# A mixture-of-experts vision kernel: who waits for the landing of the scattered rows

## The reference

```python
h = tok(x, channel_weights)            # sums of 16 x 16 patches, then 12 -> 192: 196 tokens per image
h = h + attn(layernorm(h), ...)        # 12 heads of 16; relu(1 + qk + qk*qk/2), normalised, @ v, @ w_proj + b_proj
h = h + ffn(layernorm(h), ...)         # 8 experts, top 2 of a softmax router

# ffn, for each expert e:
w_e = sum(top_w * (top_i == e))
h   = gelu(flat @ w1[e] + b1[e])       # 192 -> 768
out = out + w_e * (h @ w2[e] + b2[e])  # 768 -> 192
```

## Time and profile before

| | |
|---|---|
| median of 3 runs | 1792.08 us (1792.0 to 1793.45) |
| profiled execution | 1789.12 us, of it a span of 1787.3 us from the first to the last instruction |
| TensorE busy | 1380.5 us, 77% |
| DVE busy | 975.3 us, 55% |
| POOL busy | 821.5 us, 46% |
| ACT busy | 632.7 us, 35% |
| mean granted TensorE clock | 0.863 |
| moved by DMA | 318.36 MB, 178 GB/s over the span |

### The profile page before, as it was taken

The page is one execution under the profiler, slowest core; times in us unless marked ns, Lnnn a source line. Parts: engine busy times, 40 slices in busy tenths (PEclk is TensorE's granted clock), DMA queues, the critical chain, the costliest instruction groups (busy, mean ns, idle before and its releaser), DMA issues.

```text
span 1787.3 us, 29130 instructions
## 1 busy us (share of the span) xinstructions
PE 1380.5 (77%) x7878; PEld 1223.5 (68%) x7878; DVE 975.3 (55%) x3625; ACT 632.7 (35%) x1161; POOL 821.5 (46%) x617
## 2 busy tenths in 40 slices
PE   5456642696969787877787778777788779999996
PEld 4345532585858676767676777677677668988886
DVE  2867776457474747474747565756563322332332
ACT  1112111243433333333333343434243435555553
POOL 0011333245444445454545454545455556666555
PEclk9975555698989888888888889888889889999998
DMA  6976886487787878787878787878753645566555
GB/s 161 245 207 177 215 211 184 118 218 205 180 212 175 215 176 222 173 228 172 219 172 210 176 228 183 218 173 218 177 146 78 178 108 130 134 146 144 124 133 137
DMA packets 232822, 318.36 MB, mean 178 GB/s; under 512 B 27173, under 2 KB 205078, under 8 KB 232790
## 3 DMA queue, kind: packets, MB, share of 16 engines
q1 hardware_dynamic: 187094, 274.97, 56.8%
q0 software_dynamic: 45696, 43.02, 14.9%
HBM read 261.19 MB, written 56.72 MB: 178 GB/s over the span
## 4 chain that ended last, share of the span: by engine, by line
PE 51%; POOL 17%; DVE 14%; issue 10%; DMA 5%; ACT 2%; SPq 1%; POOLq 0%; DVEq 0%; ACTq 0%
PE ps L904 17%; PE ps L879 16%; POOL rows_d L545 10%; POOL result L560 4%; DMA rows_d<-rows,sloti 4%; DVE red L948 4%; PE ps L708 3%; PE ps L828 3%; PE ps L852 3%; PE ps L853 3%; POOL w1l L568 3%; PE ps L817 2%; DVE topi L1074 1%; PE ps L902 1%; PE ps L776 1%
## 5 line engine op out<-in xcount | busy, mean ns | idle before, releaser
L904 PE MATMUL ps<-w2r,hid 128*128 128x192 f32 x2736 | 538.7, 339 | 0.0
L904 PEld LDWEIGHTS ps<-w2r,hid 128*128 128x128 f32 x2736 | 489.6, 200 | 30.3 <-issue 1.5
L560 POOL DMA_INDIRECT result<-ys,ridx x228 | 353.6, 1551 | 277.5 <-issue 143.0
L948 DVE TENSOR_REDUCE red<-xbuf 112x14 f32<-112x448 f32 x768 | 425.8, 606 | 35.2 <-PE ps L776 34.5
L545 POOL DMA_INDIRECT rows_d<-rows,sloti x256 | 246.3, 962 | 416.1 <-DVE sloti L1124 236.1
L656 ACT ACTIVATE hid<-ps,b1s 128x512 f32<-128x512 f32 x344 | 236.0, 686 | 370.7 <-PE ps L879 369.6
L568 POOL TENSOR_TENSOR w1l<-w1r,w1h 128x768 fp32r<-128x768 f32 x116 | 238.2, 2054 | 250.4 <-ACT w1h L666 250.1
L879 PE MATMUL ps<-xh,w1h 128*128 128x512 f32 x344 | 183.8, 534 | 119.2 <-POOL w1l L568 110.5
L1170 DVE TENSOR_TENSOR xl<-ps,xh 128x512 fp32r<-128x512 f32 x58 | 40.1, 691 | 257.5 <-ACT xh L672 257.5
L879 PEld LDWEIGHTS ps<-xh,w1h 128*128 128x128 f32 x344 | 68.3, 199 | 126.6 <-issue 119.5
L776 PE MATMUL ps<-cst,red 112*48 112x14 f32 x448 | 44.7, 251 | 129.0 <-DVE red L948 112.7
(11 more groups left out here) (168 smaller groups left out, 1891.5 us busy)
## 6 DMA issues: line engine op xcount, KB each, us to landing
xbuf<-x SPq DMA_DIRECT2D x128, 1176.0 KB, 10.4
w2r<-L_ffn_w SPq DMA_DIRECT2D x177, 192.0 KB, 3.9
xr<-rows_d SPq DMA_DIRECT2D x59, 402.0 KB
w1r<-L_ffn_w SPq DMA_DIRECT2D x59, 384.0 KB, 3.4
w1r<-L_ffn_w SPq DMA_DIRECT2D x118, 192.0 KB, 4.2
result<-h1s SPq DMA_DIRECT2D x32, 294.0 KB
rows_d<-rows,sloti POOLq DMA_INDIRECT x256
result<-ys,ridx POOLq DMA_INDIRECT x228, 5.0
```

Of the source, the lines that this page charges most:

```text
L560: pool.indirect_dma_start(out, bass.IndirectOffsetOnAxis(ap=ridx[:, b, n:n + 1], axis=0), ys[:, b, n, :], None, compute_op=ALU.add).then_i ...
L904: last = mm(yout(n), hid[:, m % 3, cols], w2r[:, b, m, :], start=False, stop=m == MC - 1 and n % 2 == 1)
L948: V.tensor_reduce(red[:, k // 2, CH * (k % 2) + c, :], xbuf[:, k % XSLOTS, c, :].rearrange("p (r j w) -> p j r w", r=2, j=G), AX.XY, ALU.a ...
```

## The change

POOL no longer waits at the end of `Q` and no longer raises the two semaphores, which go. Each of the four waiters now waits on the DMA semaphores `d_scat` and `d_h1` themselves: 256 of `d_scat` and 32 of `d_h1` for each step. In step 0 ACT and DVE have nothing to wait for; for that, step 0 is written out ahead of the loop of the prologue on every engine, which makes the program longer by one copy of the step without tiles.

```diff
         def schedule(eng, handlers, prime=None, before_tail=None):
 
-            with eng.Fori(0, PRO) as s:
+            tiles_do(eng, handlers, s=0, with_tiles=False)
+            with eng.Fori(1, PRO) as s:
                 tiles_do(eng, handlers, s=s, with_tiles=False)
...
+        def after_first(s):
+
+            return not isinstance(s, int) or s > 0
...
-                sp.wait_ge(s_listed, listed)
+                wait_first(sp, d_scat, listed * (32 * NT))
+                sp.wait_ge(d_h1, listed * 32)
                 w = d_rows[buf]
...
-            with sp.Fori(0, PRO) as s:
+            tiles_do(sp, handlers, s=0, with_tiles=False)
+            with sp.Fori(1, PRO) as s:
                 tiles_do(sp, handlers, s=s, with_tiles=False)
...
-                listed[0] = s + 1
+                listed[0] = s
...
-            pool.sem_inc(s_stored, 1)
-            pool.sem_inc(s_listed, 1)
...
-                if q == 3:
-                    pool.wait_ge(d_scat, s * (32 * NT) + 32 * NT)
-                    pool.wait_ge(d_h1, s * 32 + 32)
-                    pool.sem_inc(s_stored, 1)
-                    pool.sem_inc(s_listed, 1)
...
             def S8(s, q):
                 if q == 0:
-                    act.wait_ge(s_stored, s + 1)
+                    if after_first(s):
+                        act.wait_ge(d_h1, s * 32)
...
-                    act.wait_ge(s_listed, s + 1)
+                    if after_first(s):
+                        act.wait_ge(d_scat, s * (32 * NT))
...
             def S11(s):
 
-                dve.wait_ge(s_listed, s + 1)
+                if after_first(s):
+                    dve.wait_ge(d_scat, s * (32 * NT))
```

More of the change, by code:

```diff
@@ L311, in vit_layer @@
         s_res, s_h1 = sem("residual_ready"), sem("residual_copied")
-        s_stored = sem("residual_stored")
         s_gap, s_th, s_norm = sem("gap_ready"), sem("tanh_ready"), sem("rows_normalised")
@@ L315, in vit_layer @@
         s_slots = sem("slots_ready")
-        s_listed = sem("rows_listed")
         s_pick = sem("tile_picked")
@@ L488, in _ @@
             handlers = {"P": P, "L": L, "J": J, "K": K, "S10": S10}
-            with sp.Fori(0, PRO) as s:
+            tiles_do(sp, handlers, s=0, with_tiles=False)
+            with sp.Fori(1, PRO) as s:
                 tiles_do(sp, handlers, s=s, with_tiles=False)
             for j in range(2):
-                load_rows(j, j, PRO + 1, first=True)
+                load_rows(j, j, PRO, first=True)
                 load_w1(j, j, first=True)
@@ L508, in _ @@
             sp.wait_ge(d_pad, 32 + 16 * NE)
-            listed[0] = STEPS + 1
+            listed[0] = STEPS
             with sp.Fori(0, TAIL) as i:
```

## The result

The changed kernel takes 1729.53 us (median of 4 runs, 1725.22 to 1732.18), the kernel before 1792.04 us beside it (1788.08 to 1793.45): a ratio of 0.9652, 95% interval 0.9624 to 0.9681. The forecast was 1711 us with a range of 1690 to 1745. The profiled execution took 1726.95 us, 62.2 us less than the 1789.12 us of the one before.

The account below looks back on a forecast made before the run. The prediction took POOL's wait for the scatters' landing, ahead of the adds and w1l, as the bound. Terms 69.7 + 11.7 = 81.4 us off the profiled 1789.1 gave 1707.7, plus 3.0 for the median: 1711 us, range 1690 to 1745.

Parts of the forecast that it names:

- What bounds the kernel: Twelve steps with tiles: the last scatter's landing holds POOL's adds and w1l, so TensorE waits about 8.5 us each.
- POOL's two waits go: POOL, twelve places: first add follows the last scatter by 0.40 us, saving 69.7 us, ends 70.9 and 57.9.
- an idle time of the same length before the second add: Sign on POOL that the forecast is wrong: the 4 to 8 us idle time reappears before the second add.
- its lower end of 57.9: Least saving from POOL's wait, if the first add still came 1.38 us after release at twelve places.
- TensorE's clock: TensorE after the gaps: shorter gaps keep 2.4 GHz, five places at 2.33 us give 11.7 us, ends 0 and 25.6.
- the five that the forecast had under 1.9 us: Remaining TensorE gaps before w1l taken as short enough to keep the clock, below the halfway mark of 2.1 us.
- SP's, ACT's and DVE's own waits: These engines wait for scatters and stores themselves: 0 us taken, SP's estimated 6 us of added instructions hidden.
- step 0 outside the loop: Prologue: executing one written-out copy of the step costs 0, give or take 1 us.
- What would be late next: After the change: second tile's rows with 2 us slack, DMA engines with less time per step, last 21 tiles unchanged.
- The rows of the second tile: X0 of the second tile moves earlier to 543.3 us, its rows land by about 541, slack 2 us.
- the rival in which DMA becomes the bound: Earlier adds take turns from the loads, rows land 4 to 5 us later, half the gain lost: 1751 us; chance 0.15.
- The fit for a software-generated transfer: Scatter landing at about 2.0 us plus bytes over 436 GB/s: some 2.2 us, time about 1766 us; rejected for the trace.

Follow-up runs that it names:

- Experiment 1: Changed kernel with POOL's wait for the scatters' landing at the end of Q put back, without announcements: 1808.86 us, ratio 0.9985 to the kernel before.
- experiment 2: Kernel before with only step 0 written out ahead of the loops: 1813.42 us, ratio 1.0014 to the kernel before.
- experiment 10: Changed kernel with the first half of w1l ahead of the adds of A in steps with tiles, tail in old order: 1740.87 us, ratio 0.9622.
- experiment 11: Kernel before, POOL's wait and announcements kept, first half of w1l ahead of them in steps with tiles, tail in old order: 1740.08 us, ratio 0.9617.
- experiment 6: Changed kernel with the first half of the next tile's w1l ahead of the adds of A everywhere, tail included: 1774.91 us, ratio 0.9793.
- experiment 3: Kernel before with POOL's waits and announcements moved behind the next step's first W0, step 0 in its loop: 1771.13 us, ratio 0.9771.
- experiment 4: Changed kernel with eight more adds of zeros to padding rows posted by POOL ahead of step 0: 1790.85 us, ratio 0.9880 to the kernel before.
- experiment 5: Changed kernel run again, unaltered, on the second of the three later chips: 1759.45 us, ratio 0.9697 to the kernel before.
- experiment 8: Changed kernel with TensorE doing the eight matmuls of S4 twice in steps with tiles: 1784.79 us, ratio 0.9855 to the kernel before.
- experiment 9: Changed kernel run again, unaltered, on the third of the three later chips: 1762.47 us, ratio 0.9735 to the kernel before.
- experiment 12: Changed kernel with three more adds of zeros to padding rows ahead of step 0: 1766.47 us, ratio 0.9765 to the kernel before.

## Why the prediction was right, and where it was off

**What bounds the kernel** was read rightly: the landing of the scatters was in the chain of every step with tiles, and it left it. Experiment 1 puts the whole gain on that wait.

**"POOL's two waits go", 69.7 us.** The hand-over was 0.30 us, the lower end, so the term itself gave 70.9. But the step asked only what could hold the first add, and took the remaining three for granted. In three of the twelve places POOL paused before the second add, 12.8 us in all. The paragraph on signs to look for named "an idle time of the same length before the second add" as one that would speak against the forecast; it came in three steps of twelve. The term measured 58.1 us, which is next to its lower end of 57.9, for another reason than that end was drawn from. TensorE's wait for `w1l` was forecast to fall to about 40 us; it is 55.1, and the pauses are 12.8 of that.

**"TensorE's clock", 11.7 us.** It measured 4.1. This is the step that failed. It read a gap of 1.41 us as one that keeps the clock and one of 2.76 as one that loses it, both rightly, and drew the line halfway, at 2.1 us. But nothing in the rows spoke for the middle. Gaps of 1.50, 1.66, 1.80 and 2.33 us left the first matmul at 2.4 GHz, but behind the last three the clock fell nonetheless, 1.0 to 1.5 us into the work, and cost 1.7 us each (estimates, as in the table). Only the gap of 1.50 us cost nothing. The gap of 2.42 us cost 1.7 us too, and those of 2.8 to 3.1 us cost 2.7 to 2.9, more than most gaps of about 9 us did before (1.6 to 3.1). So a gap that was cut from 9 to 3 us gave nothing back of the clock, and could take more. The gaps were mis-sized too: of the five that the forecast had under 1.9 us (steps 5, 6, 7, 9 and 11) two came so, 1.66 and 1.50 us; the others were 3.04, 7.28 (a pause) and 2.76. The price of 2.33 us a gap was right: 28.1 us behind twelve gaps before is 2.34 each.

**SP's, ACT's and DVE's own waits, and step 0 outside the loop, 0 us.** Right: experiments 1 and 2, to within their intervals. SP's added instructions cost nothing that shows there either.

**What would be late next.** The rows of the second tile were not: TensorE's other waits in the step did not grow, DMA fell to 1% of the chain, and the rival in which DMA becomes the bound (1751 us) did not come. Per microsecond DMA moved more between `S1` of step 5 and `S1` of step 15, 209 GB/s against 196 (the kernel before first):

```profile
417.57:1331.66 914.09, 726.46 (x4251) 647.27 (x4251) 562.52 (x2111) 338.85 (x630) 450.24 (x341) 0.87 0.80 196
415.82:1275.39 859.57, 721.92 (x4250) 643.56 (x4250) 580.39 (x2111) 339.08 (x630) 451.11 (x341) 0.90 0.84 209
```

The fit for a software-generated transfer of the Trainium skill (DMA: Bandwidth & Descriptors, Anatomy of one DMA) would have made the wait worth 26 us; what went before the first adds was 70.9. The trace was the right guide, since it held the landing beside full DMA engines.

**The sum** was 81.4 us against 62.2: 11.6 of the 19.2 us are the pauses (69.7 to 58.1), 7.6 the clock. The 1.2 us won in the prologue and the 1.2 us by which the lines of the table exceed the measured gain cancel. Of the last, 0.3 us are in the stretch from the last of the twelve gaps to the end (342.9 us, before 342.5); where the rest is, no view showed.

**Of the other chips** the forecast says nothing, and there the gain was 46 to 55 us in place of 62. In the step, two waits lie one behind the other on TensorE: for DVE's `phi` before `S3` and then for `w1l`. Where the first is longer, less of the second is left to be won: in experiment 2 the wait for `w1l` is 75.9 us, on the chip of the result 110.5.

## What to carry to other kernels

A wait on an engine costs what is queued behind it and is needed soonest. Before removing one, ask which instruction behind it somebody waits for, and whether that instruction can go first: here 2 us of `w1l` moved ahead of the wait were worth at least as much as removing the wait (experiments 10 and 11). But that holds per stage: the same order cost a gap of 3.1 to 4.2 us in every three tiles of the tail, and the clock behind it, where the operand of the moved work was not ready (experiment 6). And when a wait leaves a train of several transfers, price the gaps between all of them, not only the one before the first.

## What the runs showed that was not expected

**POOL's posting of transfers can pause in the middle.** With scatters just posted and not waited for, POOL stood 2.6 to 5.4 us between the first and the second add behind them, in steps 7, 10 and 13, on all four chips, in the changed kernel and in experiments 3, 4, 5, 8, 9 and 12. With `w1l` between the scatters and the adds it was 2.02 us in step 7, 2.54 in step 10 and gone in step 13 in experiment 10, and 2.78, 2.58 and 1.15 us in experiment 6. With the wait in place there was none between two adds. What it waits for can be read from the packets of POOL's own queue (q0), here in step 10 of the changed kernel, in the windows 947:948, 948:949 and 949:950 us:

```profile
q0 software_dynamic: 103, 0.14, 64.9%
q0 software_dynamic: 132, 0.11, 63.6%
q0 software_dynamic: 11, 0.01, 5.0%
```

From 950 to 951 us this queue moves nothing, and the second add starts at 951.20. In windows of 0.25 us the last packets before the second add are 1.0, 1.2 and 1.3 us ahead of it in the three pauses. In experiment 3 they are within 0.4 us of it. In step 8, which has no pause, the queue still moves 9 to 14 packets in 0.25 us when the second add starts (775.69 us). So in those three steps POOL went on only when what it had posted was through or nearly so, and the later the adds begin, the less is left of that. DVE did the same instructions during the pause of step 7 as in step 8.

The kernel before has smaller hold-ups too. The first add of a tile that waits for ACT starts 0.8 us after the end of `ys`; for the tiles 6, 19 and 31 it is 2.2 to 2.3 us, and for tile 50, in the tail, 1.6, though POOL's wait on `d_add` at the head of `A` means that the adds of the tile before had landed, and no scatter was under way. The changed kernel has them at the same tiles (the 7.1 us of the waits above is at tile 6, with the wait for `ys` in it). Not the cause of the long pauses: the longer program and instruction loads (experiment 3), and the number of transfers or rows posted before (experiments 4 and 12). Why they come every third step, and there alone, stays open. Other data or another length of the step were not tried.

**The clock can fall after the gap.** Behind gaps of 1.66, 1.80 and 2.33 us TensorE resumed at 2.4 GHz, fell to 1.2 GHz 1.0 to 1.5 us later, while it was busy, and stayed there for some 3.4 us. So the duration of the first matmul after a gap (0.49 or 0.79 us here) does not tell whether the clock was lost; the windows of the following ten microseconds do.

**The same kernel differs by over 1% from chip to chip:** the kernel before took 1792.0, 1808.6, 1811.6 and 1814.0 us, with a prologue longer by some 23 us or more on the three later chips. Ratios to the kernel before on the same chip differ as well, 0.9652, 0.9697 and 0.9735 for the same change.
